# Where the rounded upper parts of three weight blocks lie, and which loads stand ahead of which, in the opening of an adaLN transformer block

## The chip, the cores and the metric

The kernel runs on one core of one Trainium2 chip. The metric is device time of one execution in microseconds (us), the median of several runs; less is better. The engines are TensorE (PE, with its weight loads as PEld), VectorE (DVE), ScalarE (ACT), GpSimd (POOL) and SyncE (SP), which issues most transfers. Each runs its own program in order and waits for the others on semaphores.

## The reference, cut to what matters

```python
mod = silu(c) @ wmod                      # c [4, 512], wmod [512, 6*512]
sa, ca, ga, sb, cb, gb = mod, cut in six  # each [4, 1, 512]
ga, gb = sign(ga) * max(|ga|, 0.25), sign(gb) * max(|gb|, 0.25)
h = layernorm(x) * (1 + ca) + sa          # x [4, 1024, 512]
x = x + ga * attention(h, Wq, Wk, Wv, Wo) # 16 heads, scores of rank 64 common to all heads, softmax
h = layernorm(x) * (1 + cb) + sb
x = x + gb * (sum over r of h @ factors[r] / sqrt(8) + bias)
```

The scores are the same for all heads, so that attention is one matrix of probabilities per batch entry, and Wv and Wo can be multiplied into one matrix ahead of it.

## The kernel before, in words

x is 32 tiles of 128 tokens, two tiles to a pair, eight tiles to a batch entry. Products in float32 are made from two rounded parts: an upper part (a rounded copy, made by ScalarE with `rounded`) and a rest (whole minus upper, made by VectorE with `rest`). A product is then three matmuls (`three`, lines 467 to 472): upper by lower, lower by upper, upper by upper. The opening makes everything that depends on weights alone and the first eight tiles' queries, keys and values; then `step(t)` runs for t from 0 to 31, each with one tile of attention, one of feed-forward and one of a later tile's projection.

The opening, in each engine's own order:

SyncE (lines 348 to 373) loads Wv and Wo by quarters, the columns of Wmod for SA and CA by quarters (`wmod_0`), the first x, Wqk and x's pair 1. It then waits for the sums of SA and CA (`mod_acc`), loads the columns for GA and SB (1024 KB each, `load_vector`), x's pair 2, the first factor (`f_sum`), pair 3, the columns for CB and GB, waits for GA's sum (line 368), and loads pairs 4 and 5 and the bias. `load_x(pair)` (line 303) waits, for every pair but the first, until all earlier pairs have landed. After that come the gate's rows and the steps.

TensorE (lines 689 to 721) begins with eight matmuls on zeros (`WARMUPS`, line 691), then the terms of Wv times Wo (`weights_term(k, i, j)`: quarter k, with upper or lower parts i and j) between the sums of SA and CA (`early_upper`, `early_rest`), then the columns of SA and CA (`modulation_columns`, which turns rows of the sums to columns), x's first tile (`transpose_x(0)`), the last quarter (`weights_last(3)`), and four `prep_pair` with the sums of GA, SB and CB (`modulation`) in between. In `prep_pair(p)` TensorE transposes tiles 2p+1 and 2p+2, projects queries and keys of the pair (`project_qk`) and the values of its two tiles.

ScalarE (lines 984 to 1052) makes the exponential for silu, the upper parts of all weights (`wv_upper`, `wo_upper`, `vector_upper(v, k)`, line 943), the normalized rows of x (`x_row`), h (`h_of`) and the upper parts of values, queries and keys. Around the change its order is: `vector_upper(SB, 1)`, `x_row(4)`, `vector_upper(SB, 2)`, `vector_upper(CB, 0)`, `values_of(2)`, `h_of(4)`, `x_row(5)`, `vector_upper(SB, 3)`, `qk(1)`, `vector_upper(CB, 1)`, `h_of(5)`, `x_row(6)`.

VectorE (lines 1317 to 1447) makes silu, all rests (`vector_rest`, `wv_rest`, ...), the statistics of x (`moments_of`), and rounds h (`h_first`, `h_second`). Around the change: `qk_rest(1)`, `moments_of(8)`, `vector_rest(CB, 0)`, `h_first(5)`, `h_second(5)`.

GpSimd (lines 1550 to 1607) makes the inverse deviations (`of_x`, which waits for ScalarE's earlier row of x) and issues the loads that add factors 1 to 7 onto `f_sum` in memory, each in two halves; a half waits for the landing of the same half before it.

The parts of the weights lie under tiles that are used later. `w_part_0` lies where x's pairs 4 and 5 go, `w_part_1` where pairs 6 and 7 go; `w_part_4` is where the raw columns of GA land, once SA's rests are used. The lists of line 160 and 161 say which block's parts lie in which `w_part`. Lines 943 to 955 and 1288 to 1294 wait until the block that lay there before is done with.

Of the kernel before, what the change touches and what calls it, by code (L numbers as in the profile page):

```python
# [8 lines left out]
ALU = mybir.AluOpType  # L9
AX_X = mybir.AxisListType.X  # L10

P = 128
EPS = 1e-5
GATE_FLOOR = 0.25
SA, CA, GA, SB, CB, GB = range(6)
WARMUPS = 8
LO_ROW = 32
# [41 lines left out]
def adaln_block(nc, x, wqk_t, wv, wo_t, factors, bias, c_t, wmod, out):  # L59
# [19 lines left out]
    B = c_t.shape[1] // (D // P)  # L79
    C = D // P  # L80
# [17 lines left out]
    with ExitStack() as ctx:  # L98
        def sb(name, shape, dt=F32, stack=ctx):
            return stack.enter_context(nc.sbuf_tensor(name, shape, dt))  # L100

        def bank(name, columns=D):
            return ctx.enter_context(nc.psum_tensor(name, [P, columns], F32))

        def sem(name):
            return ctx.enter_context(nc.semaphore(name))
# [3 lines left out]
        silu_parts = sb("silu_parts", [P, C, LO_ROW + B], F32R)  # L110
# [39 lines left out]
        with ExitStack() as setup:  # L150
            sb("under_parts", [P, TB, D], F32, setup)
            w_parts = [sb("w_part_0", [P, C, D], F32R, setup), sb("w_part_1", [P, C, D], F32R, setup)]
# [4 lines left out]
        with ExitStack() as setup:  # L157
            sb("under_f", [P, 6 * TB * D + 2 * KEYS + 2 * C * P + 4 * D + C * D + C * P + 4 * P + D], F32, setup)
            f_sum = sb("f_sum", [P, C, D], F32, setup)
        w_hi = [w_parts[i] for i in (0, 1, 0, 1, 4, 1)]  # L160
        w_lo = [w_parts[i] for i in (4, 5, 2, 3, 2, 3)]

        x_ring = sb("x_ring", [P, 2 * TB, D])
# [19 lines left out]
        probs = sb("probs", [P, KEYS])  # L183
        early = C * (LO_ROW + B)
        no_parts = probs[:, 0:early].rearrange("p (c n) -> p c n", c=C)
        c_sb, silu_den, silu_c = [probs[:, early + C * B * i:early + C * B * (i + 1)].rearrange("p (c b) -> p c b", c=C)
                                  for i in range(3)]

        ps_s = bank("ps_s", KEYS)
        ps_t = [bank("ps_t0"), bank("ps_t1")]  # L190
# [31 lines left out]
        consts_set = sem("consts_set")  # L222
        ident_set = sem("ident_set")
        silu_exp, silu_steps = sem("silu_exp"), sem("silu_steps")
        weights_hi_done, weights_lo_done = sem("weights_hi_done"), sem("weights_lo_done")
        wv_late_done = sem("wv_late_done")
        w_hi_done = [sem(f"w_hi_done{v}") for v in range(6)]
        w_lo_done = [sem(f"w_lo_done{v}") for v in range(6)]
        low_copied = sem("low_copied")
        mod_acc = sem("mod_acc")  # L230
# [31 lines left out]
        def wait(eng, semaphore, value):  # L262

            if not isinstance(value, int) or value > 0:
                eng.wait_ge(semaphore, value)

        def wait_alone(eng, passed, semaphore, value):


            eng.wait_ge(semaphore, value)  # L270
            eng.sem_inc(passed, 1)
# [4 lines left out]
        def full(ap):  # L276

            return ap.bitcast(F32)
# [9 lines left out]
        def mod_row(i):  # L288

            return pb[0:B].rearrange("b s (r d) -> b (s r) d", d=D)[:, i, :]  # L290
# [11 lines left out]
        def _(sp):  # L302
            def load_x(pair):
                if not isinstance(pair, int) or pair > 0:
                    wait_alone(sp, sp_passed, x_loaded, pair * 16)
                slot = (pair & (2 * PB - 1)) * 2
                sp.dma_start(x_ring[:, bass.ds(slot, 2), :], x_pairs[pair]).then_inc(x_loaded, 16)
# [18 lines left out]
            def load_vector(v):  # L326
                to = (wmod_1 if v < CB else wmod_2)[:, v % 2]
                sp.dma_start(to, wmod[:, D * v:D * (v + 1)].rearrange("(k p) n -> p k n", p=P)).then_inc(vector_loaded[v], 16)
# [34 lines left out]
            load_x(2)  # L363
            sp.dma_start(f_sum[:], factors[0].rearrange("(c p) n -> p c n", p=P)).then_inc(f0_loaded, 16)
            load_x(3)
            load_vector(CB)
            load_vector(GB)
            sp.wait_ge(mod_acc, GA + 1)
            load_x(4)
            load_x(5)  # L370
            sp.dma_start(bias_bc[:], bias.partition_broadcast(P)).then_inc(bias_loaded, 16)
            store_gate(0, GA)
            spread_gate(0, 0)
# [92 lines left out]
        def _(pe):  # L466
# [38 lines left out]
            def modulation_columns(n, vectors):  # L505
                for i, v in enumerate(vectors):
                    for k in range(C):
                        at = (i * C + k) * B
                        last = nc.tensor.transpose(mod_t_banks[n][:, at:at + B], mod_row(row_of[v])[:, P * k:P * (k + 1)],
                                                   ident[0:B, 0:B])  # L510
                last.then_inc(mod_tps, 1)

            def transpose_x(q, acc=ps_t[1], rows=xn):
                pe.wait_ge(xn_done, q + 1)
                wait(pe, h_f_done, q)
                transposes(acc, rows, C).then_inc(xt_ps, 1)
# [132 lines left out]
            def wv_rest_in(k):  # L649
                if k < 2:  # L650
                    pe.wait_ge(weights_lo_done, 2 * k + 1)
                else:
                    pe.wait_ge(wv_late_done, k - 1)
# [4 lines left out]
            def weights_term(k, i, j):  # L658

                pe.wait_ge(weights_hi_done, 2 * k + 2)  # L660
                if i:
                    wv_rest_in(k)
                if j:
                    wo_rest_in(k)
                for m in range(C):
                    nc.tensor.matmul(wvo_banks[m][:], wv_parts[i][:, k, P * m:P * (m + 1)], wo_parts[j][:, k, :],
                                     start=(k == 0 and i == 0 and j == 0), stop=False)
# [20 lines left out]

            pe.wait_ge(consts_set, 2)
            for _ in range(WARMUPS):  # L690
                nc.tensor.matmul(ps_t[0][0:LO_ROW + B, 0:C * (LO_ROW + B)], no_parts[:, 0, :],
                                 no_parts.rearrange("p c n -> p (c n)"), start=True, stop=True)
            weights_term(0, 0, 0)
            weights_term(0, 1, 0)
            weights_term(0, 0, 1)
# [11 lines left out]
            weights_term(1, 0, 1)  # L707
            weights_term(2, 0, 0)
            weights_term(2, 1, 0)
            weights_term(2, 0, 1)  # L710
            pe.wait_ge(ident_set, 2)
            pe.wait_ge(rows_done, 2)
            modulation_columns(0, (SA, CA))
            transpose_x(0)
            weights_last(3)
            prep_pair(0)
# [26 lines left out]
        def _(act):  # L743
# [199 lines left out]
            def vector_upper(v, k):  # L943

                if v in (SA, CA):
                    act.wait_ge(wmod_loaded[k], 16)
                else:
                    act.wait_ge(vector_loaded[v], 16)
                if v in (GA, SB):
                    act.wait_ge(mod_acc, CA + 1)  # L950
                elif v == CB:
                    act.wait_ge(w_lo_done[GA], C)
                elif v == GB:
                    act.wait_ge(mod_acc, SB + 1)
                rounded(w_hi[v][:, k, :], raw(v, k)).then_inc(w_hi_done[v], 1)

            def low_row(v):
# [5 lines left out]
            def wv_upper(k):  # L963
                act.wait_ge(wv_loaded[k], 16)
                rounded(wv_parts[0][:, k, :], wv_raw[:, k, :]).then_inc(weights_hi_done, 1)

            def wo_upper(k):
                act.wait_ge(wo_loaded[k], 16)
                rounded(wo_parts[0][:, k, :], wo_raw[:, k, :]).then_inc(weights_hi_done, 1)
# [12 lines left out]
                values(q, prologue_v[q % 2])  # L982

            act.dma_start(probs[:, early:early + C * B], c_t).then_inc(c_loaded, 16)
            act.wait_ge(c_loaded, 16)
            nc.scalar.activation(silu_den, c_sb, ACT.Exp, scale=-1.0).then_inc(silu_exp, 1)
            wv_upper(0)
            wo_upper(0)
            for k in range(C):
                vector_upper(SA, k)  # L990
                vector_upper(CA, k)
# [86 lines left out]
        def _(dve):  # L1078
            def rest(to, whole, hi):

                return nc.vector.tensor_tensor(to, whole, full(hi), ALU.subtract)  # L1081
# [202 lines left out]
            def wo_rest(k):  # L1284
                dve.wait_ge(weights_hi_done, 2 * k + 2)
                rest(wo_parts[1][:, k, :], wo_raw[:, k, :], wo_parts[0][:, k, :]).then_inc(weights_lo_done, 1)
# [30 lines left out]
            nc.vector.memset(minus_half[:], -0.5).then_inc(consts_set, 1)  # L1317
            nc.vector.memset(no_parts, 0.0).then_inc(consts_set, 1)

            dve.wait_ge(silu_exp, 1)  # L1320
            nc.vector.tensor_scalar(silu_den, silu_den, 1.0, None, ALU.add).then_inc(silu_steps, 1)
            dve.wait_ge(silu_steps, 1)
            nc.vector.reciprocal(silu_den, silu_den).then_inc(silu_steps, 1)
            dve.wait_ge(silu_steps, 2)
            nc.vector.tensor_tensor(silu_c, c_sb, silu_den, ALU.mult).then_inc(silu_steps, 1)

            dve.wait_ge(consts_set, 2)
            nc.vector.tensor_copy(silu_parts[:], no_parts).then_inc(silu_steps, 1)
            dve.wait_ge(silu_steps, 4)
            nc.vector.tensor_copy(silu_parts[:, :, 0:B], silu_c).then_inc(silu_steps, 1)  # L1330
            dve.wait_ge(silu_steps, 5)
            rest(silu_parts[:, :, LO_ROW:], silu_c, silu_parts[:, :, 0:B]).then_inc(silu_steps, 1)
            rows = [0]

            def row(v):
# [33 lines left out]

            wv_rest(0)  # L1370
            wo_rest(0)
            for k in range(C):
                vector_rest(SA, k)
                vector_rest(CA, k)
                if k == 1:
                    wv_rest(1)
                    wo_rest(1)
# [272 lines left out]
```

## Time and profile before

| | before |
|---|---|
| median of 3 runs | 468.11 us (466.95 to 468.57) |
| the profiled execution, its own time | 465.86 us |
| its span | 464.1 us |
| busy share of the span: PE, PEld, DVE, ACT, POOL | 97%, 79%, 79%, 73%, 52% |
| share of the 16 DMA engines' span: hardware queue of SP, software queue of POOL | 56.1%, 9.1% |

How to read it: the span is the stretch that the profile covers; the profiled execution's own time is that of the whole launch, so it is a little longer than the span. The profiled execution is one more run beside the three of the median. Busy time counts what an engine executes; matmuls are pipelined, so that TensorE's busy time overlaps itself, and its waits are read from the waits and the order of time, not from the share. Idle time on an engine other than the one that sets the pace costs nothing by itself.

### The profile page before, as it was taken

What the parts mean: (1) busy time and instruction counts of PE and PEld (TensorE: products, weight loads), DVE (VectorE), ACT (ScalarE), POOL (GpSimd) and SP (SyncE); (2) the same over time, 40 slices, a digit from 0 to 9 for tenths busy, and PEclk for the clock granted to TensorE, in tenths of its full rate; (3) what the DMA queues carried; (4) which work ended last, traced back from release to release, by engine and by line L of the source; (5) the groups of instructions that cost most, each with busy time, mean ns of one, the idle gap of its engine ahead of it and who ended that gap; (6) DMA issues with size and microseconds to landing.
All of it is one profiled execution on the core that took longest, in us unless ns stands there. A gap on an engine that the chain in (4) does not pass through costs nothing. (4 is left out here: it accounts for less than half of the span.)

```text
span 464.1 us, 7353 instructions
## 1 busy us (share of the span) xinstructions
PE 450.8 (97%) x2116; PEld 364.9 (79%) x2116; DVE 364.6 (79%) x639; ACT 338.3 (73%) x676; POOL 239.8 (52%) x309
## 2 busy tenths in 40 slices
PE   8999999999999999999999999999999989999996
PEld 5677778788888888788888888888788867777674
DVE  5887978678787988788887887788786678786765
ACT  5899677687878697778886886888687476566551
POOL 0545745162545634455565645455464576566662
PEclk9999999999999999999999999999999999999999
DMA  8999998624678365877776366868674237575612
GB/s 291 348 354 225 178 174 166 149 72 135 181 219 256 93 201 163 246 216 230 217 224 205 115 200 185 268 181 240 188 226 124 90 115 216 170 220 173 188 55 91
DMA packets 79176, 88.07 MB, mean 190 GB/s; under 512 B 4888, under 2 KB 55832, under 8 KB 79136
## 3 DMA queue, kind: packets, MB, share of 16 engines
q1 hardware_dynamic: 75040, 79.99, 56.1%
q0 software_dynamic: 3808, 7.34, 9.1%
q8 instruction: 17, 0.28, 0.2%
q10 hardware_dynamic: 288, 0.27, 0.2%
q14 instruction: 23, 0.19, 0.1%
HBM read 53.49 MB, written 34.10 MB: 189 GB/s over the span
## 5 line engine op out<-in xcount | busy, mean ns | idle before, releaser
L470 PE MATMUL ps_o<-v_lo,pt_hi 128*128 128x512 f32 x256 | 100.2, 392 | 0.8 <-DVE pt_lo L1081 0.7
L472 PE MATMUL ps_o<-v_hi,pt_hi 128*128 128x512 f32 x256 | 99.7, 389 | 0.0
L471 PE MATMUL ps_o<-v_hi,pt_lo 128*128 128x512 f32 x256 | 99.6, 389 | 0.0
L1489 POOL TENSOR_SCALAR ve<-mv 128x1 f32<-128x1 f32 x64 | 22.5, 352 | 149.1 <-DVE mv L1192 116.5
L470 PEld LDWEIGHTS ps_o<-v_lo,pt_hi 128*128 128x128 f32 x256 | 48.0, 188 | 12.9 <-issue 3.0
L1081 DVE TENSOR_TENSOR h_lo<-h_f,h_hi 128x512 fp32r<-128x512 f32 (+1 forms) x67 | 46.8, 699 | 13.2 <-ACT h_hi L745 13.0
L472 PEld LDWEIGHTS ps_o<-v_hi,pt_hi 128*128 128x128 f32 x256 | 48.0, 188 | 10.1
L471 PEld LDWEIGHTS ps_o<-v_hi,pt_lo 128*128 128x128 f32 x256 | 48.1, 188 | 9.6
L773 ACT ACTIVATE h_f<-x1b,mod_t 128x128 f32<-128x128 f32 x120 | 53.1, 596 | 3.4 <-DVE x1b L1210 3.2
L470 PE MATMUL ps_y<-f_lo,h_hi 128*128 128x512 f32 (+1 forms) x124 | 48.6, 392 | 2.0 <-ACT ffn L882 1.0
L773 ACT ACTIVATE h_f<-xb,mod_t 128x128 f32<-128x128 f32 x80 | 35.4, 594 | 17.6 <-DVE xb L1206 17.6
L472 PE MATMUL ps_y<-f_hi,h_hi 128*128 128x512 f32 (+1 forms) x124 | 47.9, 386 | 0.0
L471 PE MATMUL ps_y<-f_hi,h_lo 128*128 128x512 f32 (+1 forms) x124 | 47.9, 386 | 0.0
L1491 POOL TENSOR_TENSOR rstd<-ve,minus_half 128x1 f32<-128x1 f32 x64 | 44.7, 699 | 5.3
L470 PE MATMUL ps_v<-wvo_lo,h_hi 128*128 128x512 f32 x112 | 44.3, 396 | 0.0
L471 PE MATMUL ps_v<-wvo_hi,h_lo 128*128 128x512 f32 x112 | 43.8, 391 | 0.0
L1215 DVE STREAM_TRANSPOSE pb<-pb 128x1024 f32<-128x1024 f32 x24 | 29.8, 1241 | 17.7 <-DMA pb<-p_blocks 17.7
L472 PE MATMUL ps_v<-wvo_hi,h_hi 128*128 128x512 f32 x112 | 43.6, 389 | 0.0
L1506 POOL TENSOR_TENSOR ffn<-ffn,bias_bc 128x512 f32<-128x512 f32 x29 | 39.9, 1374 | 5.2 <-ACT ffn L882 5.2
L1516 POOL TENSOR_TENSOR x_ring<-ffn,x_ring 128x512 f32<-128x512 f32 x30 | 39.0, 1300 | 5.2 <-POOL ffn L1512 5.0
L1512 POOL TENSOR_TENSOR ffn<-ffn,gates 128x512 f32<-128x512 f32 x29 | 39.0, 1344 | 5.1 <-issue 5.1
L1140 DVE TENSOR_REDUCE negmax<-ps_s 128x1 f32<-128x1024 f32 x32 | 38.8, 1212 | 1.9 <-PE ps_s L547 1.5
(202 smaller groups left out, 1036.7 us busy)
## 6 DMA issues: line engine op xcount, KB each, us to landing
x_blocks<-xn SPq DMA_DIRECT2D x50, 256.0 KB, 2.8
p_blocks<-probs SPq DMA_DIRECT2D x24, 512.0 KB, 3.8
pb<-p_blocks SPq DMA_DIRECT2D x96, 128.0 KB, 3.3
x_ring<-in_x SPq DMA_DIRECT2D x15, 512.0 KB, 3.9
x1b<-x_blocks SPq DMA_DIRECT2D x30, 256.0 KB, 2.8
result<-x_ring SPq DMA_DIRECT2D x15, 512.0 KB, 3.1
f_sum<-in_factors POOLq DMA_DIRECT2D x14, 512.0 KB, 6.0
xb<-x_blocks SPq DMA_DIRECT2D x20, 256.0 KB, 3.1
```

The lines of the kernel that those rows point to most:

```text
L470: nc.tensor.matmul(acc, a_hi, b_lo, start=first, stop=False)
L471: nc.tensor.matmul(acc, a_lo, b_hi, start=False, stop=False)
L472: return nc.tensor.matmul(acc, a_hi, b_hi, start=False, stop=last)
L773: last = nc.scalar.activation(to[:, k, :].rearrange("p (c b) -> p b c", b=Q), turned[:, k], ACT.Identity, scale=mod_t[:, b, v + 1, k:k + 1 ...
L1081: return nc.vector.tensor_tensor(to, whole, full(hi), ALU.subtract)
L1140: nc.vector.tensor_reduce(negmax[:, t & 3:(t & 3) + 1], ps_s[:], AX_X, ALU.max, negate=True).then_inc(max_done, 1)
L1215: nc.vector.transpose(pb[:, n & 1, :], pb[:, n & 1, :]).then_inc(pb_turned, 1)
L1489: nc.gpsimd.tensor_scalar(ve[:, one], mv[:, u, 1:2], EPS, None, ALU.add).then_inc(ve_done, 1)
L1491: nc.gpsimd.tensor_tensor(rstd[:, one], ve[:, one], minus_half[:], ALU.pow).then_inc(rstd_done, 1)
L1506: nc.gpsimd.tensor_tensor(ffn[:], ffn[:], bias_bc[:], ALU.add).then_inc(biased_done, 1)
L1512: nc.gpsimd.tensor_tensor(ffn[:], ffn[:], gates[:, 1, b & 1, :], ALU.mult).then_inc(gated_done, 1)
L1516: nc.gpsimd.tensor_tensor(tile, ffn[:], tile, ALU.add).then_inc(y_done, 1)
```

## The change

Block SA keeps `w_part_0` for its upper part, GA's goes from `w_part_0` to `w_part_1`, SB's from `w_part_1` to `w_part_4`, CB's from `w_part_4` to `w_part_1`. With that `w_part_0` is used by SA alone, and x's pairs 4 and 5 are loaded right behind pair 3, ahead of CB and GB; the bias, which lies where a quarter of Wo lay, waits for the rests of Wo. The waits ahead of the upper parts follow the new homes. The dummy matmuls take 128 stationary columns instead of 36. The columns of SA and CA come ahead of `weights_term(2, 0, 1)`. The exponential on ScalarE goes behind the first two roundings, and silu on VectorE behind the first two rests.

```diff
-        w_hi = [w_parts[i] for i in (0, 1, 0, 1, 4, 1)]
+        w_hi = [w_parts[i] for i in (0, 1, 1, 4, 1, 1)]
         w_lo = [w_parts[i] for i in (4, 5, 2, 3, 2, 3)]
...
             load_x(3)
+            load_x(4)
+            load_x(5)
             load_vector(CB)
             load_vector(GB)
-            sp.wait_ge(mod_acc, GA + 1)
-            load_x(4)
-            load_x(5)
+            sp.wait_ge(weights_lo_done, 6)
             sp.dma_start(bias_bc[:], bias.partition_broadcast(P)).then_inc(bias_loaded, 16)
             store_gate(0, GA)
...
             for _ in range(WARMUPS):
-                nc.tensor.matmul(ps_t[0][0:LO_ROW + B, 0:C * (LO_ROW + B)], no_parts[:, 0, :],
-                                 no_parts.rearrange("p c n -> p (c n)"), start=True, stop=True)
+                nc.tensor.matmul(ps_t[0][:, 0:early], probs[:, 0:P], probs[:, 0:early], start=True, stop=True)
...
             weights_term(2, 1, 0)
-            weights_term(2, 0, 1)
             pe.wait_ge(ident_set, 2)
             pe.wait_ge(rows_done, 2)
             modulation_columns(0, (SA, CA))
+            weights_term(2, 0, 1)
             transpose_x(0)
...
-                if v in (GA, SB):
+                if v == GA:
                     act.wait_ge(mod_acc, CA + 1)
+                elif v == SB:
+                    act.wait_ge(w_lo_done[GA], C)
                 elif v == CB:
-                    act.wait_ge(w_lo_done[GA], C)
+                    act.wait_ge(mod_acc, GA + 1)
                 elif v == GB:
-                    act.wait_ge(mod_acc, SB + 1)
+                    act.wait_ge(mod_acc, CB + 1)
                 rounded(w_hi[v][:, k, :], raw(v, k)).then_inc(w_hi_done[v], 1)
...
             act.dma_start(probs[:, early:early + C * B], c_t).then_inc(c_loaded, 16)
+            wv_upper(0)
+            wo_upper(0)
             act.wait_ge(c_loaded, 16)
             nc.scalar.activation(silu_den, c_sb, ACT.Exp, scale=-1.0).then_inc(silu_exp, 1)
-            wv_upper(0)
-            wo_upper(0)
...
-            dve.wait_ge(silu_exp, 1)
-            nc.vector.tensor_scalar(silu_den, silu_den, 1.0, None, ALU.add).then_inc(silu_steps, 1)
...
-            rest(silu_parts[:, :, LO_ROW:], silu_c, silu_parts[:, :, 0:B]).then_inc(silu_steps, 1)
             rows = [0]
...
             wv_rest(0)
             wo_rest(0)
+            dve.wait_ge(silu_exp, 1)
+            nc.vector.tensor_scalar(silu_den, silu_den, 1.0, None, ALU.add).then_inc(silu_steps, 1)
...
+            rest(silu_parts[:, :, LO_ROW:], silu_c, silu_parts[:, :, 0:B]).then_inc(silu_steps, 1)
             for k in range(C):
                 vector_rest(SA, k)
```

## Rows read from the trace of the kernel before

**Rows 1.** The page: TensorE's busy time, share of the span, instructions, and the rest.

```profile
PE 450.8 (97%) x2116; PEld 364.9 (79%) x2116; DVE 364.6 (79%) x639; ACT 338.3 (73%) x676; POOL 239.8 (52%) x309
```

**Rows 2.** Waits of TensorE up to 110 us: us in total, times, longest.

```profile
PE ps_qk L470 <- DVE h_lo L1081: 1.6, 1, 1.6
```

**Rows 3.** TensorE in order of time: start us, us, instruction, idle before and releaser.

```profile
41.62 0.60 PE L476 MATMUL ps_t<-ident,xn 128*128 128x128 f32 x4
...
44.80 0.60 PE L476 MATMUL ps_t<-ident,xn 128*128 128x128 f32 x4
47.03 0.39 PE L470 MATMUL ps_qk<-h_lo,wqk_hi 128*128 128x256 f32 x1 [1.63 <-DVE h_lo L1081]
```

**Rows 4.** VectorE in order of time, around the ninth tile's statistics.

```profile
44.22 0.70 DVE L1084 BATCH_NORM_STATS2 stats<-x_ring 128x6 f32<-128x512 f32 x1 [2.08 <-DMA x_ring<-in_x]
...
46.29 0.69 DVE L1081 TENSOR_TENSOR h_lo<-h_f,h_hi 128x512 fp32r<-128x512 f32 x1
```

**Rows 5.** SyncE in order of time: pair 3, CB and GB, pairs 4 and 5.

```profile
25.95 0.37 SPq L307 DMA_DIRECT2D x_ring<-in_x  x1
26.36 1.02 SPq L328 DMA_DIRECT2D wmod<-in_wmod  x2
34.51 10.14 SPq L307 DMA_DIRECT2D x_ring<-in_x  x2
```

**Rows 6.** Issues, us to landing: pair 1, GA, pair 3, CB, pair 4, pair 5.

```profile
x_ring<-in_x SPq DMA_DIRECT2D x1, 512.0 KB, 3.5
...
wmod<-in_wmod SPq DMA_DIRECT2D x1, 1024.0 KB, 5.8
...
x_ring<-in_x SPq DMA_DIRECT2D x1, 512.0 KB, 6.2
...
wmod<-in_wmod SPq DMA_DIRECT2D x1, 1024.0 KB, 8.5
...
x_ring<-in_x SPq DMA_DIRECT2D x1, 512.0 KB, 9.7
...
x_ring<-in_x SPq DMA_DIRECT2D x1, 512.0 KB, 5.2
```

**Rows 7.** ScalarE in order of time, around CB's first rounding.

```profile
35.95 1.17 ACT L745 ACTIVATE w_part<-wmod 128x512 fp32r<-128x512 f32 x2
...
39.07 0.84 ACT L759 ACTIVATE xn<-x_ring,nmr,rstd 128x512 f32<-128x512 f32 x1
```

**Rows 8.** GpSimd in order of time: the first accumulating loads.

```profile
30.73 2.64 POOL L1572 DMA_DIRECT2D f_sum<-in_factors  x2 [0.27 <-issue]
...
40.93 1.25 POOL L1572 DMA_DIRECT2D f_sum<-in_factors  x1 [3.49 <-DMA f_sum<-in_factors]
```

**Rows 9.** DMA queues, 39 to 40 and 46 to 47 us: packets, MB, share of engines.

```profile
q1 hardware_dynamic: 69, 0.14, 40.5%
q0 software_dynamic: 67, 0.13, 69.5%
...
q1 hardware_dynamic: 181, 0.37, 97.1%
q0 software_dynamic: 9, 0.01, 7.1%
```

**Rows 10.** TensorE in order of time, two of the first products of weights.

```profile
6.11 0.63 PE L666 MATMUL ps_y<-v_hi 128*128 128x512 f32 x1
6.53 0.48 PE L666 MATMUL ps_qk<-v_hi 128*128 128x512 f32 x1
```

**Rows 11.** ScalarE in order of time, the first rows of Wmod.

```profile
7.65 2.40 ACT L745 ACTIVATE w_part<-wmod 128x512 fp32r<-128x512 f32 x4 [2.70 <-DMA wmod<-in_wmod]
```

**Rows 12.** TensorE in order of time: columns, transposes, last product of weights.

```profile
18.84 0.66 PE L509 MATMUL ps_t<-ident,pb 4*128 4x4 f32 x8
19.43 0.66 PE L476 MATMUL ps_t<-ident,xn 128*128 128x128 f32 x4
20.53 0.47 PE L470 MATMUL ps_v<-v_lo,v_hi 128*128 128x512 f32 x1 [0.45 <-DVE v_lo L1081]
```

More of the change, by code:

```diff
@@ L1318, in _ @@
             nc.vector.memset(no_parts, 0.0).then_inc(consts_set, 1)
-            dve.wait_ge(silu_exp, 1)
-            nc.vector.tensor_scalar(silu_den, silu_den, 1.0, None, ALU.add).then_inc(silu_steps, 1)
[L1322 to L1331, printed above, removed]
-            rest(silu_parts[:, :, LO_ROW:], silu_c, silu_parts[:, :, 0:B]).then_inc(silu_steps, 1)
             rows = [0]
@@ L1371, in _ @@
             wo_rest(0)
+            dve.wait_ge(silu_exp, 1)
+            nc.vector.tensor_scalar(silu_den, silu_den, 1.0, None, ALU.add).then_inc(silu_steps, 1)
+            dve.wait_ge(silu_steps, 1)
+            nc.vector.reciprocal(silu_den, silu_den).then_inc(silu_steps, 1)
+            dve.wait_ge(silu_steps, 2)
+            nc.vector.tensor_tensor(silu_c, c_sb, silu_den, ALU.mult).then_inc(silu_steps, 1)
+            dve.wait_ge(consts_set, 2)
+            nc.vector.tensor_copy(silu_parts[:], no_parts).then_inc(silu_steps, 1)
+            dve.wait_ge(silu_steps, 4)
+            nc.vector.tensor_copy(silu_parts[:, :, 0:B], silu_c).then_inc(silu_steps, 1)
+            dve.wait_ge(silu_steps, 5)
+            rest(silu_parts[:, :, LO_ROW:], silu_c, silu_parts[:, :, 0:B]).then_inc(silu_steps, 1)
             for k in range(C):
```

## The prediction

> **What bounds the kernel now.** I read the page first: TensorE is busy for 97% of the span [rows 1], so a stage ahead of the steady part is worth what TensorE waits in it, and a delay there is carried to the end. Next came the list of waits up to 110 us: the longest that TensorE has after its first matmul is 1.6 us, on line 470, for h_lo [rows 2]. TensorE's order of time puts it between 44.80 us and 47.03 us, ahead of the third pair's query and key projection [rows 3]. VectorE's order of time says why: the statistics of x's ninth tile start at 44.22 us after 2.08 us of waiting for the load of x_ring, and h_lo, which follows them on VectorE, starts only at 46.29 us [rows 4]. SyncE issues that load, x's fifth pair, at 34.51 us [rows 5], 9.7 us ahead of its landing [rows 6], because it first waits for GA's sum. This is the wait at which the change aims.
>
> The other side is ScalarE. The row at 35.95 us is two roundings, SB's third and CB's first [rows 7]; at 0.58 us apiece CB's starts near 36.5 us. CB was issued at 26.36 us [rows 5] and took 8.5 us [rows 6], so it was there at 34.9 us, 1.6 us early. Behind it on ScalarE stand the values of tile 2, h of tile 4 and x's row 5 (39.07 us) [rows 7], which TensorE takes at 41.62 us [rows 3]. So CB's first rounding has little to spare.
>
> **The change part by part.**
>
> *The early loads of x.* It issues the same transfers in another order. Loading pair 4 waits for the landing of pair 3, and loading pair 5 for that of pair 4; CB and GB, which were issued right behind pair 3, now stand behind both waits on SyncE. The gain: VectorE's 2.08 us and with it TensorE's 1.6 us. The price is CB's new landing, in four terms.
> 1. Pair 3 is issued at 25.95 us and landed 6.2 us later, at 32.15 us, with CB and GB pressing behind it [rows 5, 6]. An undisturbed pair (pair 1, the second) took 3.5 us [rows 6], which would give 29.45 us. It still has f_sum's first megabyte ahead of it, so I take 31.5, near the late end.
> 2. Pair 4 takes from 3.5 us (that pair) to 9.7 us (its own row before). POOL issues the first two accumulating loads from 30.73 us on, and the first lands only when the wait at 40.93 us ends [rows 8], so pair 4 shares the engines with them. I take the 5.2 us of pair 5 before [rows 6], which also ran beside accumulations with little of its own queue ahead: landed at 36.7 us.
> 3. CB is issued some 0.4 us later (the length of pair 5's issue), at 37.1 us, behind 512 KB. GA stood exactly so behind the second pair and took 5.8 us [rows 6]: the early end. For the late end, between 39 and 40 us the hardware queue moved 69 packets and the accumulating one 67 [rows 9]; pair 5 and CB are 768 packets of 2 KB, 11.1 us at that pace, about 13 with start and receipt. The opposite shows from 46 to 47 us, with 181 packets against 9 [rows 9]. I take the middle, 9.4 us, because POOL runs out of accumulations to issue while ScalarE stands (its moments of x's row 7 wait for ScalarE's row 5). CB lands at 46.5 us.
> 4. From CB's first rounding to TensorE's projection was 10.5 us (36.5 to 47.03 us), of which 2.1 were the wait that goes: 8.4 remain. So the projection starts at 46.5 + 8.4 = 54.9 us, 7.9 us later than before. It breaks even where CB lands at 38.6 us.
>
> TensorE would then stand from 41.6 us to about 50. After its start it ran slow: two matmuls of 512 columns stand 0.42 us apart there [rows 10], the pace of its 1.2 GHz level (512 columns in 0.43 us), against 12 such matmuls and four transposes in 3.18 us later on, from 41.62 to 44.80 us [rows 3]. If it resumes slow, the twelve that follow the gap take 5.0 us, some 2 more, part of it beside work that it awaits anyway: bounds 0 and 2, I take 0.8, below the middle for that reason.
>
> *The homes of GA, SB and CB.* No instruction more or less. GA keeps its wait. SB's upper part now waits for GA's last rest, which stands on VectorE right behind the first half of h of tile 2; ScalarE has a row of x, a key copy and two value tiles between. CB's waits for GA's sum, over when SyncE's wait for the same event ended, at 34.5 us [rows 5], ahead of 36.5; GB's waits for CB's sum, for which ScalarE has already waited to copy its low row. Nothing, as long as those stand ahead; up to a rounding's half microsecond if not.
>
> *SyncE's wait for the low weights* is over long before it is reached; the bias behind it moves up, the gate's store waits for its rows as before. Nothing.
>
> *Silu behind the first rests, the exponential behind two roundings.* ScalarE then waits 2.70 us for Wmod's first rows until 7.65 us [rows 11], which sets the early sums, so what is gained before it is lost there. The silu's six short VectorE instructions, which move behind two rests, fit into the same gap: nothing. Without that cover it would be the length of one rounding.
>
> *Wider dummies.* 128 stationary columns instead of 36 with the same 144 moving ones: if the load of weights hides, nothing; if the clock rises sooner, the matmuls at 0.42 us gain up to 0.2 us each for a few, below 1 us; if it shows, as much is lost. Either is swallowed by the wait to 7.65 us.
>
> *Columns ahead of a term.* The columns begin at 18.84 us, right behind the terms, the transposes of x's first tile at 19.43 us, and the last product waits 0.45 us for VectorE's last rest and starts at 20.53 us [rows 12]. Four matmuls, 1 us at the pace of rows 3, go from ahead of the columns to between them and the transposes. Where the rows that the columns read are there by then, the columns and the rest behind them on VectorE come up to 1 us sooner and the wait of 0.45 us goes; where TensorE has to wait for the rows, the transposes come up to 1 us later, and with them ScalarE's h. I take 0, the middle of 0.45 won and some 0.5 lost, and CB's landing, which follows from SyncE's chain, covers both. If CB is in time, that shift shows.
>
> Sum: 7.9 + 0.8 = 8.7 us. The profiled execution took 465.86 us, 2.25 below the median of 468.11: 474.6 there, 476.8 on the median.
>
> **The rivals.**
> *Transfers undisturbed.* The hardware queue gets its way, as from 46 to 47 us [rows 9]: pair 3 at 31.5, pair 4 3.5 us, CB 0.4 + 5.8 us, landed at 41.2 us: 2.6 us lost, 470.7 us. For it speaks that row, against it the row at 39 us. The Trainium skill (DMA: Bandwidth & Descriptors, Anatomy of one DMA) fits a transfer on the software path as 2.0 us plus its bytes at 436 GB/s; by that estimate pair 4 takes 3.2 us and CB behind pair 5 5.6 us, and the time would be about 470. The rows of 3.5 and 5.8 us agree with it, that of 9.7 us doesn't.
>
> *Transfers shared throughout.* Pair 4 7 us, CB 13 us, landed near 52 us: 13.4 us and 1.5 for the clock, 483 us. For it speaks the row at 39 us; against it, that POOL stops feeding accumulations. The Trainium skill (the same page, Queues, rings and completion order) says that each engine goes round robin between the queues that have work, by packets; 69 against 67 agrees with it, 181 against 9 shows a time when one had next to none. By that rule alone this rival is what happens.
>
> *CB in time: faster.* The place is ScalarE's first rounding of CB. If it lands by 38.6 us nothing is lost, by 37 us the whole 1.6 us are won: 466.5 us. That asks pair 3 at 29.45, pair 4 in 3.5 us and CB in under 5.3 us, all at or under the quickest rows. A lookalike is that the late x isn't what VectorE waits for; its row names the load, so I give that nothing of its own.
>
> **How the numbers follow.** Chances: the forecast (CB landing from 43 to 51 us, 472.5 to 482) 0.57; undisturbed (468.5 to 472.5) 0.23; shared throughout 0.10; faster 0.10. About what a measurement can tell from no change is 0.3%, 1.4 us; of the undisturbed case 0.05 lies within it. So 0.10 faster, 0.05 same, 0.85 slower. The range runs from 469.0, which takes in most of the undisturbed case, to 483.0, where the shared one begins; some 0.2 lies outside.
>
> **What would show it.** Right: TensorE has a wait of 5 to 10 us between 41 and 52 us that follows back to ScalarE's w_part and to Wmod's load; VectorE's wait for x_ring is gone; x's pair 4 is issued near 31.5 us and CB near 37 us; the projection starts near 55 us and the stretch from there to the end is as long as before. Wrong: CB issued by 33 us, or ScalarE without a wait for Wmod after 30 us; then the span falls by some 1.6 us. If the projection is late but the end is not, a wait further back had room that I did not see.

## The result, and the profile after

The changed kernel took 477.03 us (median of four runs, 473.34 to 483.38), the kernel before on the same chip 467.53 us (four runs, 466.83 to 468.57): a ratio of 1.0175, 95% interval 1.0105 to 1.0246, a loss of 9.5 us between the medians. The ratio leaves out the longest of the four, 483.38 us, because it lies more than 1.5% above the shortest; the median of the other three is 475.87 us, a loss of 8.3 us. The profiled execution is that longest one (span 481.6), so its stretch behind the opening is read beside a second profile of the same kernel (the run `after_again`, span 473.3).

The page of the changed kernel, its line of engines (in place of [rows 1]) and its row of granted TensorE clock in 40 slices of 12 us:

```profile
PE 454.4 (94%) x2116; PEld 367.4 (76%) x2116; DVE 362.7 (75%) x639; ACT 338.2 (70%) x676; POOL 241.2 (50%) x309
...
PEclk9998799999999999999999999999999999999999
```

The same 2116 matmuls as before, in a span 17.5 us longer; the clock dips to eight and seven tenths only in the fourth and fifth slice, from 36 to 60 us. The waits up to 110 us (in place of [rows 2]; us in total, times, longest) say what is new there:

```profile
ACT w_part L744 <- DMA wmod<-in_wmod: 12.1, 5, 9.5
...
PE ps_t L476 <- ACT xn L758: 8.0, 2, 7.6
```

Three long waits hang on each other: TensorE waits for ScalarE's row of x, VectorE for ScalarE's h (9.7 us), and ScalarE for Wmod. The load that comes late is found on SyncE. First its order of time (start, us, instruction; in place of [rows 5]), then the landings (in place of [rows 6]): pair 3, pair 4, pair 5 and CB.

```profile
25.17 9.60 SPq L307 DMA_DIRECT2D x_ring<-in_x  x3
34.82 1.33 SPq L328 DMA_DIRECT2D wmod<-in_wmod  x2
```

```profile
x_ring<-in_x SPq DMA_DIRECT2D x1, 512.0 KB, 5.4
...
x_ring<-in_x SPq DMA_DIRECT2D x1, 512.0 KB, 3.7
...
x_ring<-in_x SPq DMA_DIRECT2D x1, 512.0 KB, 7.1
...
wmod<-in_wmod SPq DMA_DIRECT2D x1, 1024.0 KB, 10.9
```

The three pairs of x, with the two waits between them, take SyncE from 25.17 to 34.77 us, so CB is issued at 34.82 us; before it was 26.36 us. What ScalarE, VectorE and TensorE make of that, in their order of time (start, us, instruction, in brackets the idle time before and what ended it; in place of [rows 7], [rows 4] and [rows 3]):

```profile
35.62 0.65 ACT L744 ACTIVATE w_part<-wmod 128x512 fp32r<-128x512 f32 x1
45.79 0.63 ACT L744 ACTIVATE w_part<-wmod 128x512 fp32r<-128x512 f32 x1 [9.51 <-DMA wmod<-in_wmod]
```

```profile
51.15 0.68 DVE L1085 BATCH_NORM_STATS2 stats<-x_ring 128x6 f32<-128x512 f32 x1
```

```profile
49.05 1.12 PE L476 MATMUL ps_t<-ident,xn 128*128 128x128 f32 x4 [7.60 <-ACT xn L758]
50.01 0.79 PE L470 MATMUL ps_t<-wvo_lo,h_hi 128*128 128x512 f32 x1
...
51.03 0.63 PE L472 MATMUL ps_t<-wvo_hi,h_hi 128*128 128x512 f32 x1
51.45 0.63 PE L470 MATMUL ps_t<-wvo_lo,h_hi 128*128 128x512 f32 x1
...
55.24 0.36 PE L470 MATMUL ps_qk<-h_lo,wqk_hi 128*128 128x256 f32 x1
```

SB's third rounding stands alone at 35.62 us, where before CB's followed at once. ScalarE then waits 9.51 us for CB, with the values of tile 2, h and the row of x queued behind it. VectorE's statistics of the ninth tile, at 51.15 us behind the rest of the second pair's queries and keys, no longer wait for x_ring: the wait at which the change aimed is gone, and a longer one has come. The projection, at 47.03 us before, starts at 55.24 us.

The windows from 45 to 55 us (us; busy time of five engines; granted clock, share of the DMA engines, GB/s) show the clock:

```profile
45.00:50.00 5.00, 0.95 (x4) 0.72 (x4) 1.67 (x4) 4.19 (x10) 0.00 (x0) 0.50 1.09 263
50.00:55.00 5.00, 5.00 (x15) 3.92 (x15) 4.58 (x11) 4.62 (x10) 2.88 (x6) 0.56 0.41 123
```

After standing from 41.5 to 49 us TensorE resumes at 0.50, the 1.2 GHz level: its matmuls of 512 columns start 0.42 us apart (51.03 and 51.45 us), and the twelve from 50.01 us end at the transposes of 54.88 us. From 55 to 60 us the clock is at 1.00 again.

Last, why CB took about 11 us. The queues' packets, MB and share of the 16 engines, from 34.5 to 38 us, 38 to 40, 40 to 43 and 43 to 46 us (in place of [rows 9]), and GpSimd's order of time (in place of [rows 8]):

```profile
q0 software_dynamic: 358, 0.70, 111.6%
...
q1 hardware_dynamic: 2, 0.00, 0.3%
...
q0 software_dynamic: 124, 0.23, 63.0%
q1 hardware_dynamic: 150, 0.31, 44.5%
...
q1 hardware_dynamic: 598, 1.19, 101.9%
...
q0 software_dynamic: 196, 0.40, 72.0%
q1 hardware_dynamic: 196, 0.37, 38.0%
```

```profile
30.41 2.64 POOL L1573 DMA_DIRECT2D f_sum<-in_factors  x2 [0.27 <-issue]
...
38.40 1.25 POOL L1573 DMA_DIRECT2D f_sum<-in_factors  x1 [1.28 <-DMA f_sum<-in_factors]
...
41.31 1.25 POOL L1573 DMA_DIRECT2D f_sum<-in_factors  x1 [0.23 <-issue]
51.10 0.23 POOL L1490 TENSOR_SCALAR ve<-mv 128x1 f32<-128x1 f32 x1 [8.53 <-DVE mv L1089]
```

CB's 11 us fall into four stretches. Up to 38 us the hardware queue (q1), on which pair 5 and CB had been issued, moved next to nothing while the accumulating queue (q0) moved most of its first two half loads. Then the two shared, from 40 to 43 us the hardware queue had the engines to itself, and from 43 us on, when the half loads that GpSimd issued at 38.40 and 41.31 us came in, they moved packet for packet. GpSimd itself stood for want of moments only behind those two issues. Why the hardware queue moved nothing at first is not shown.

### The profile page after: what moved, and what is told of

Its sections match the earlier page's. It is cut to its first block and busy times, and to the rows that moved or that the text cites. A ratio compares the mean times of both kernels' runs of the same rounds, so it can differ in the third digit from the quotient of the medians.

```text
span 481.6 us, 7353 instructions
## 1 busy us (share of the span) xinstructions
PE 454.4 (94%) x2116; PEld 367.4 (76%) x2116; DVE 362.7 (75%) x639; ACT 338.2 (70%) x676; POOL 241.2 (50%) x309
## 5 line engine op out<-in xcount | busy, mean ns | idle before, releaser
L1082 DVE TENSOR_TENSOR h_lo<-h_f,h_hi 128x512 fp32r<-128x512 f32 (+1 forms) x67 | 46.6, 696 | 12.7 <-ACT h_hi L744 12.4
```

## The experiments

Each ratio is against runs of the kernel before on the same chip. All kernels but `order_alone` start from the changed kernel; none leaves work out.

**The changed kernel again** (`after_again`, no edit).

> The changed kernel once more, for its own spread and a second profile. Late CB (the forecast): median 474 to 478 us, ScalarE waits 8 to 11 us for Wmod's CB, the third pair's projection starts at 53 to 56 us. What the first profile lost beyond that, some 10 us between 110 and 290 us in waits for h_lo: if it belongs to that one execution, the lag behind the kernel before stays at 7 to 9 us from 80 us to the end here; if the change makes the steps themselves slower, the lag grows again to 12 us or more.

475.61 us (six runs), ratio 1.0188 [1.0141, 1.0236]. ScalarE in order of time, and TensorE's projection:

```profile
46.58 0.63 ACT L744 ACTIVATE w_part<-wmod 128x512 fp32r<-128x512 f32 x1 [10.39 <-DMA wmod<-in_wmod]
```

```profile
56.28 0.36 PE L470 MATMUL ps_qk<-h_lo,wqk_hi 128*128 128x256 f32 x1
```

The same picture. What the opening costs TensorE is read from a row that every profile has, transposes of probabilities in an early step: before, then the changed kernel's first profile.

```profile
100.02 1.06 PE L476 MATMUL ps_t<-ident,probs 128*128 128x128 f32 x8 [0.23 <-issue]
```

```profile
107.81 1.06 PE L476 MATMUL ps_t<-ident,probs 128*128 128x128 f32 x8 [0.23 <-issue]
```

In the second profile they start at 108.91 us, so TensorE is 7.8 and 8.9 us late there. Behind it the two differ. Taking the stores of results one by one (the first comes at 137.84 us in the profile of before), this execution is 9.3 us behind at the first and 9.2 us at the last; the first profile is 9.5 us behind there, 19.0 us at 264 us and 17.5 us near the end. What it lost on the way are waits of TensorE for h_lo in the steps, 8.7 us from 110 us on against 1.3 us before and 0.9 us here. So in this execution the whole loss is made in the opening and carried to the end, and the medians, 8.3 us without the longest run and 9.4 us, say that this is the usual case. That the steps' own losses have nothing to do with a late opening is not shown: between the first store and the last, the four other profiles with a late opening (`order_alone`, `adds_held` and the two of `kept_busy`) fall back by a further 3.3 to 6.0 us, the six without one by at most 2.2 us.

**The order of loads alone** (`order_alone`: the kernel before, with the new homes, which the order needs because pairs 4 and 5 land on `w_part_0`, their waits, and the new order; dummies, columns and silu as before).

```diff
             load_x(3)
+            load_x(4)
+            load_x(5)
             load_vector(CB)
             load_vector(GB)
-            sp.wait_ge(mod_acc, GA + 1)
-            load_x(4)
-            load_x(5)
+            sp.wait_ge(weights_lo_done, 6)
```

> The kernel before with only the new homes and the new order of loads; dummies, columns, silu and the exponential as before. If the order alone makes the loss: CB lands at 45 to 48 us, TensorE waits 7 to 9 us at tile 5, the time is 474 to 477 us as with the whole change. If the other edits take part in it: below 472 us.

476.85 us (four runs), 1.0225 [1.0157, 1.0293]: the whole loss. ScalarE waits 10.73 us for CB until 46.46 us.

**All but the order** (`old_order`: the changed kernel with the old order and the old wait).

```diff
             load_x(3)
-            load_x(4)
-            load_x(5)
             load_vector(CB)
             load_vector(GB)
-            sp.wait_ge(weights_lo_done, 6)
+            sp.wait_ge(mod_acc, GA + 1)
+            load_x(4)
+            load_x(5)
```

> The changed kernel with the old order of loads and the old wait for GA's sum; homes, dummies, columns, silu stay changed. Late CB: those edits are worth nothing, 467 to 469 us, and the wait of 1.6 us for h_lo is back. Rival (one of them costs): above 470 us.

466.77 us (twelve runs), 1.0000 [0.9966, 1.0034]. With the run before it this puts the loss on the order: homes, dummies, columns and silu together are worth nothing that can be measured. But the wait of 1.6 us for x was not back. Pair 4, issued at 33.88 us, with its landing, and VectorE's order of time:

```profile
x_ring<-in_x SPq DMA_DIRECT2D x1, 512.0 KB, 7.9
```

```profile
41.87 0.70 DVE L1085 BATCH_NORM_STATS2 stats<-x_ring 128x6 f32<-128x512 f32 x1 [0.32 <-POOL nmr L1494]
```

Pair 4 took 7.9 us here, not 9.7 [rows 6], landed at 41.8 us, and VectorE lost 0.32 us. So part of the wait that the change was to remove may belong to the one execution profiled before.

**Pairs 4 and 5 behind CB and GB, or behind CB only** (`x_behind_both` and `cb_first`; the second is shown).

```diff
             load_x(3)
+            load_vector(CB)
             load_x(4)
             load_x(5)
-            load_vector(CB)
             load_vector(GB)
```

> The changed kernel, with x's pairs 4 and 5 issued behind CB and GB again, but without the wait for GA's sum (the new homes stay). Late CB: CB is issued near 25.5 us and lands by 36 us, ScalarE's wait of 9.5 us is gone, pair 4 is issued near 31 us and lands at 40 to 44 us; 466 to 468.5 us, some 9 below the changed kernel. Rival (the homes, the dummies or the moved steps cost the time): 474 to 478 us as with the change.

> The changed kernel, issued in the order pair 3, CB, pairs 4 and 5, GB. Late CB: CB lands by 36 us, pair 4 near 37 us, so that neither ScalarE waits for CB nor VectorE for x; TensorE's 1.6 us of the kernel before go too: 465 to 467 us. Rival (the homes or the moved steps cost the time): 474 to 478 us. Rival (x was not what VectorE waited for): as the kernel before, 467 to 469 us, with a wait at the same projection.

467.02 us, 1.0008 [0.9976, 1.0041], and 466.03 us, 0.9998 [0.9964, 1.0032], twelve runs each. CB's place alone decides: one line moved up takes the whole loss away. In `cb_first` neither ScalarE waits for CB nor VectorE for x (ScalarE and TensorE in order of time):

```profile
35.70 1.17 ACT L744 ACTIVATE w_part<-wmod 128x512 fp32r<-128x512 f32 x2
```

```profile
44.94 0.36 PE L470 MATMUL ps_qk<-h_lo,wqk_hi 128*128 128x256 f32 x1
```

The projection starts 2.1 us sooner than before (some 0.7 us of it because this execution's loads began sooner), yet the total is that of before. The transposes of probabilities start at 97.73 us, so TensorE is still 2.3 us ahead there; at 139.71 us it waits 0.79 us for h_lo, and most of the lead is gone. VectorE shows why: x, which a step sends through memory and back, returns only 0.36 us sooner than before (before, then `cb_first`).

```profile
136.10 0.71 DVE L1206 STREAM_TRANSPOSE xb<-xb 128x512 f32<-128x512 f32 x1 [0.97 <-DMA xb<-x_blocks]
```

```profile
135.74 0.71 DVE L1207 STREAM_TRANSPOSE xb<-xb 128x512 f32<-128x512 f32 x1 [2.41 <-DMA xb<-x_blocks]
```

SyncE, which issues these transfers in order, had stood 5.4 us between storing probabilities and loading them back (116.80 to 122.21 us), against 4.0 us before (118.79 to 122.80 us). What made that landing longer is not shown. The stores are 0.3 us ahead at 137.84 us, 2.3 us behind at 239.56 us and 0.2 us ahead near the end. In `x_behind_both` pair 4 was issued at 31.79 us and in time, but VectorE's statistics, at 44.06 us, waited 1.09 us for GpSimd's inverse deviations.

**CB late as before the edit, but used later** (`cb_used_late`: the changed order; CB's first three upper parts on ScalarE, shown, and its first two rests on VectorE in the same way moved behind h of tile 6).

```diff
             vector_upper(SB, 2)
-            vector_upper(CB, 0)
             values_of(2)
...
             qk(1)
-            vector_upper(CB, 1)
             h_of(5)
...
             values_of(3)
+            h_of(6)
+            vector_upper(CB, 0)
+            qk(2)
+            vector_upper(CB, 1)
+            x_row(7)
             vector_upper(CB, 2)
-            h_of(6)
-            qk(2)
-            x_row(7)
             values_of(4)
```

> The changed kernel with its order of loads; CB's first three upper parts on ScalarE and their rests on VectorE are moved some 8 us further back (behind h of tile 6), where nothing of CB is needed yet by others. If the time went because ScalarE waits in order at CB's first rounding: CB still lands near 46 us, but TensorE no longer waits 8 us at tile 5 (under 2 us in all ahead of the third pair's projection, which starts at 45 to 48 us), and the time is 465 to 468 us. Rival (the late transfers cost the time in another way, or the homes do): still above 472 us.

466.18 us (ten runs), 1.0012 [0.9969, 1.0055]. ScalarE and TensorE in order of time:

```profile
47.67 0.63 ACT L744 ACTIVATE w_part<-wmod 128x512 fp32r<-128x512 f32 x1 [1.06 <-DMA wmod<-in_wmod]
```

```profile
44.66 0.36 PE L470 MATMUL ps_qk<-h_lo,wqk_hi 128*128 128x256 f32 x1
```

CB lands as late as in the changed kernel, and the projection no longer depends on it. What cost 9 us was not the late load but the work queued behind it on ScalarE. (The edit moves VectorE's rests of CB too, but VectorE's long wait in the changed kernel was for ScalarE's h.)

**The loads issued without waiting for each other** (`not_in_turn`: pairs 4 and 5 on semaphores of their own; the readers wait on those).

```diff
-                if not isinstance(pair, int) or pair > 0:
-                    wait_alone(sp, sp_passed, x_loaded, pair * 16)
                 slot = (pair & (2 * PB - 1)) * 2
+                if pair in x_early:
+                    sp.dma_start(x_ring[:, bass.ds(slot, 2), :], x_pairs[pair]).then_inc(x_early[pair], 16)
+                    return
+                wait_alone(sp, sp_passed, x_loaded, (pair if pair < 4 else pair - 2) * 16)
```

> The changed kernel, but x's pairs 4 and 5 have semaphores of their own, so that SyncE issues pair 3, pairs 4 and 5, CB and GB without waiting for landings in between. If the waits in turn (and the accumulations that get in meanwhile) make CB late: all are issued by 28 us, CB lands at 36.5 to 39 us, ScalarE waits 0 to 2.5 us for it, and the time is 465.5 to 468 us. Rival (the bytes of two pairs ahead of CB are enough): CB lands after 42 us, 470 us or more.

468.03 us (twelve runs), 1.0032 [0.9994, 1.0069]. CB is issued at 27.31 us, lands 9.1 us later, at 36.4 us, and ScalarE rounds it in its turn, the second of two roundings without a wait from 36.12 us on; then VectorE waits for something else (its order of time):

```profile
43.83 0.69 DVE L1088 BATCH_NORM_STATS2 stats<-x_ring 128x6 f32<-128x512 f32 x1 [1.53 <-POOL nmr L1501]
```

The same order of transfers without the two landings awaited has no loss that can be measured, and CB lands 9.4 us sooner than in the changed kernel (45.8 us). So without the serial waits on SyncE CB is nearly in time (34.9 us before). And behind the wait for x stood another: GpSimd's deviations, which wait on GpSimd behind an accumulating load.

**Deviations ahead of the accumulating loads** (`rows_first`: `not_in_turn`, and GpSimd's rows 6 and 7 each ahead of a half of factor 2).

```diff
-            add_half(2, 0)
             of_x(6, 0)
-            add_half(2, 1)
+            add_half(2, 0)
             of_x(7, 1)
+            add_half(2, 1)
```

> The kernel in which x's pairs don't wait in turn, and POOL makes the deviations of x's rows 6 and 7 ahead of the two halves of an accumulating load that they stood behind. If those halves were what the ninth tile's statistics waited for (1.5 us, by way of POOL): that wait and TensorE's 1.1 us at the projection go, and the projection starts at 45 to 45.7 us after an issue of pair 3 near 25.9. The time: at most 1.1 us lower, 465.5 to 468 us, within what the steps spread. If ScalarE's or VectorE's own work sets the projection: still beyond 46.4 us.

466.32 us (twelve runs), 1.0014 [0.9981, 1.0047]. Both waits are gone, the projection starts at 45.16 us, the stores are 1.6 to 2.3 us ahead up to 190 us, and from 264 us on within 0.9 us of before. A gain in the opening again, and again none at the end that can be told.

**Accumulating loads held until CB has landed** (`adds_held`).

```diff
-            add_factor(1)
             of_x(4, 0)
             of_x(5, 1)
+            pool.wait_ge(vector_loaded[CB], 16)
+            add_factor(1)
             add_half(2, 0)
```

> The changed kernel with POOL's accumulating loads held back until CB has landed, so that x's pairs and CB have the DMA engines to themselves. It is judged by CB's landing and the projection, since the held loads come late for the steps. If the accumulations take half of CB's lateness: pair 4 lands in 3.5 to 4 us, CB at 40 to 42 us, the projection starts at 48.5 to 51 us. If the chain of waits on SyncE alone makes CB late: CB lands at 44 us or later and the projection stays beyond 53 us.

474.91 us, one run. CB was issued at 34.13 us, as late as in the changed kernel, but landed much sooner. The landings of pair 4, of CB and of pair 5, and ScalarE in order of time:

```profile
x_ring<-in_x SPq DMA_DIRECT2D x1, 512.0 KB, 3.4
...
wmod<-in_wmod SPq DMA_DIRECT2D x1, 1024.0 KB, 5.9
x_ring<-in_x SPq DMA_DIRECT2D x1, 512.0 KB, 3.6
```

```profile
40.02 0.63 ACT L744 ACTIVATE w_part<-wmod 128x512 fp32r<-128x512 f32 x1 [3.97 <-DMA wmod<-in_wmod]
```

5.9 us for CB in place of 10.9: without the accumulating loads CB is there 5.8 us sooner, at 40.02 us. This is no second half beside the 9.4 us of `not_in_turn`, for CB was 10.9 us later than before [rows 5, 6]: the two overlap. The serial waits move CB's load into the stretch in which the accumulating loads run, and both are needed for the whole lateness. One part of it can be seen at the start: x's pair 5, issued at 33.71 us, has its first rows under way at 34.99 us here; in the changed kernel it was issued at 34.40 us and has them at 37.89 us. TensorE's first wait falls to 2.07 us. The part of the expectation on the projection missed (52.49 us): the hold stops GpSimd's deviations too, for which ScalarE waits 3.2 us and VectorE 4.28 us further on. The total therefore says nothing of CB.

**TensorE kept busy in the gap** (`kept_busy`, and the same kernel again, `kept_busy_again`: 32 matmuls of 512 columns, whose result nobody reads, ahead of the transposes of tile 5).

```diff
+            def keep_busy(n):
+                for _ in range(n):
+                    nc.tensor.matmul(ps_s[:, 0:D], wvo_hi[:, 0, 0:P], wvo_hi[:, 0, :], start=True, stop=True)
...
                 for u in range(2):
+                    if pair == 2 and u == 0:
+                        keep_busy(32)
                     transpose_x(2 * pair + u + 1)
```

> The changed kernel with 32 matmuls of 512 columns added on TensorE where it waits for x's row 5, into a bank that nobody reads then. If the resumption at the lower clock costs time: the granted clock stays at 1.00 from 45 to 55 us, the twelve matmuls behind the gap take 2.8 us instead of 4.9, the projection starts 1 to 1.7 us sooner after CB's landing (8.2 us behind it, set by h_lo) and the time is 1 to 1.7 us below the changed kernel. If h_lo decides anyway: the same time, the projection still 9 to 10 us behind CB's landing.

> The kernel with 32 added matmuls once more. If its 479 us was the spread of the steps: a median of 473 to 476.5 us now, at or below the changed kernel's, and a lag behind the kernel before that stays at 7 to 9 us through the steps. If the added matmuls themselves slow the steps: 478 us or more again, and a lag that grows by 3 us or more between 110 and 290 us.

479.11 us, 1.0284 [1.0217, 1.0351], and 480.64 us, 1.0318 [1.0272, 1.0365], six runs each. The windows, ScalarE and TensorE of the first:

```profile
50.00:55.00 5.00, 4.21 (x20) 3.02 (x20) 4.68 (x11) 4.92 (x11) 1.76 (x3) 1.00 0.64 183
```

```profile
47.22 0.63 ACT L750 ACTIVATE w_part<-wmod 128x512 fp32r<-128x512 f32 x1 [10.19 <-DMA wmod<-in_wmod]
```

```profile
55.32 0.39 PE L470 MATMUL ps_qk<-h_lo,wqk_hi 128*128 128x256 f32 x1 [0.23 <-DVE h_lo L1088]
```

With the clock at 1.00 the projection comes 8.1 us behind CB's rounding; in the changed kernel it was 9.45 and 9.70 us (45.79 to 55.24, 46.58 to 56.28). So the slow clock cost some 1.4 to 1.6 us in the opening. The total missed: by the medians 2 to 5 us more than the changed kernel's two sets, not less. In the first profile the stores are 8.5 us behind at the first, less than in `after_again`, and 14 us near the end, through waits for h_lo in the steps; the second profile goes from 10.4 to 12.9 us. In the second CB also came later (48.39 us), and TensorE stood for 3.2 us behind the 32, at a clock of 0.77 from 50 to 55 us. The interval of the second lies above that of `after_again`, that of the first overlaps it; the second set came out as expected of matmuls that slow the steps themselves (478 us or more, a lag that grows by 3 us or more). But `order_alone`, which has none of them, fell back as much in its profile (10.4 us at the first store, 13.9 near the end), so this is not shown, and why the steps lose more here is open.

## Why the prediction was right

The forecast was 476.8 us against 468.11, 8.7 us lost; measured were 477.03 us and, between medians of one set, 9.5 us (8.3 us without the longest run). TensorE alone, at the transposes of probabilities, was 7.8 and 8.9 us late. Its mechanism is what the runs show: order alone makes the loss, taking ScalarE's queue off CB takes it away. The terms were less good than the sum. From the rows above, the changed kernel and its second profile:

| term | forecast | first profile | second |
|---|---|---|---|
| pair 3 landed, us | 31.5 | 25.17 + 5.4 = 30.6 | 25.36 + 5.5 = 30.9 |
| pair 4 under way | 5.2 | 3.7 | 3.8 |
| CB issued | 37.1 | 34.8 | 35.2 |
| CB, issue to rounding | 9.4 | 11.0 | 11.4 |
| CB's first rounding | 46.5 | 45.8 | 46.6 |
| from there to the projection | 8.4 + 0.8 | 9.45 | 9.70 |
| projection | 55.7 | 55.2 | 56.3 |

*Pair 4* was mis-sized: I took that it shares with accumulations because GpSimd issues them at 30.7 us. They were issued at 30.41 us, but no packet of that queue moved before 33.58 us, so pair 4, landed at 34.4 us, went almost undisturbed, like pair 1 [rows 6]. *CB* was mis-sized the other way: for 9.4 us I let GpSimd run dry, and it had two more half loads to issue first, at 38.40 and 41.31 us, whose packets shared the engines from 43 us on; and the prediction had no stretch in which the hardware queue stands, as it did up to 38 us. CB was issued 2.3 and 1.9 us sooner than forecast, of which 0.8 and 0.6 us are only that these executions issued pair 3 sooner than the profile before (25.95 us), and it took 1.6 and 2.0 us longer. The two errors nearly cancel: that the total came so close is partly luck. The bounds of each held.

The Trainium skill (DMA: Bandwidth & Descriptors, Queues, rings and completion order) has each engine go round robin between queues with work, packet by packet. 196 packets against 196 from 43 to 46 us agree, if the profile's pieces of 2 KB are batched alike on both queues (a packet there is a batch of descriptors); 2 against 358 up to 38 us, with pair 5 and CB issued, does not look like it. The Trainium skill (the same page, Anatomy of one DMA) fits its software path with a start and a rate that make 3.2 us, as an estimate, for 512 KB. x's pairs go by the hardware queue: 3.4 and 3.6 us with the accumulating loads held come near that, 7.1 us for pair 5 beside them doesn't.

*The clock*: 0.8 us taken within 0 to 2, and 1.4 to 1.6 us measured. The cover that I named, other work awaited, was thinner: in the second profile h_lo was ready at 54.62 us and the projection waited until 56.28 us for the matmuls ahead of it.

*Columns ahead of a term*: taken as 0, between 0.45 won and 0.5 lost; it is the lost end. Count from SyncE's issue of GA's columns, from which the rest of the start keeps its distance in the profiles. The changed kernel's SyncE and TensorE (columns, transposes of tile 0, of tile 2), then those of `order_alone`, which has the old start:

```profile
15.26 1.02 SPq L328 DMA_DIRECT2D wmod<-in_wmod  x2
```

```profile
17.59 0.63 PE L509 MATMUL ps_t<-ident,pb 4*128 4x4 f32 x8 [0.34 <-DVE pb L1328]
...
19.18 0.60 PE L476 MATMUL ps_t<-ident,xn 128*128 128x128 f32 x4
...
26.70 0.66 PE L476 MATMUL ps_t<-ident,xn 128*128 128x128 f32 x4 [0.42 <-ACT xn L758]
```

```profile
15.13 1.02 SPq L328 DMA_DIRECT2D wmod<-in_wmod  x2
```

```profile
17.98 0.66 PE L509 MATMUL ps_t<-ident,pb 4*128 4x4 f32 x8
...
18.56 0.66 PE L476 MATMUL ps_t<-ident,xn 128*128 128x128 f32 x4
...
26.15 0.66 PE L476 MATMUL ps_t<-ident,xn 128*128 128x128 f32 x4 [0.29 <-ACT xn L759]
```

The columns come 2.33 us behind that issue, not 2.85, the first transposes 3.92, not 3.43, and tile 2's transposes 11.44, not 11.02: 0.4 us later, through ScalarE, as the prediction said of the case in which TensorE has to wait for the rows. It does, 0.34 us. In all eleven profiles with the new start tile 2's transposes come 11.44 to 11.47 us behind that issue, in the two with the old one 11.00 and 11.02. The total is too coarse for it, and `old_order`'s 1.0000 holds both. The homes, silu, the bias and the dummies at nothing: the first weight product starts at 4.93 us and started at 5.08 us, and no wait on their semaphores shows.

The rivals: undisturbed transfers had pair 4 right and CB wrong; shared throughout was nearer with CB (13 us taken, 11 measured) than that, though no nearer than the forecast, and had pair 4 wrong. "CB in time" didn't happen, and `cb_first`, which makes it happen, shows at 0.9998 that its 1.6 us would not have been measured either.

## What to carry to other kernels

Before moving a load behind others, ask which engine consumes it in order, and what stands behind that consumer: price the landing first, then the queue behind it. A load that is issued behind two awaited landings pays both, and whatever another queue brings in meanwhile: here CB landed 9.4 us sooner without the two waits, and 5.8 us sooner with the other queue held. A wait seen in one execution may be in part that execution's own, and behind it the next producer may be nearly as late: here the 1.6 us to win were never seen at the end.

## What was not expected

- Accumulating loads that GpSimd issued at 30.41 us moved no packet until 33.58 us. Then they had the engines nearly to themselves up to 38 us, although pair 5 and CB had been issued on the other queue at 34.40 and 34.82 us; a 1 MB load took 10.9 us beside them and 5.9 us without.
- A gain of some 2 us in the opening (`cb_first`, `rows_first`) is lost again before the end, in waits of TensorE for h_lo that fall at other steps in each execution. In `cb_first` the first of them follows transfers of x and of probabilities through memory, which come back hardly sooner than before; why they do was not settled.
- Filling the 8 us in which TensorE stands kept the granted clock at 1.00 in one profile and gained 1.4 to 1.6 us there, and yet the medians of two sets of six runs are 2 to 5 us longer than the changed kernel's.
